# Attention scores as three fp16 products, with a tile's normalisation moved on VectorE

## The reference

```python
q, k, v = h @ Wq, h @ Wk, h @ Wv        # h = layernorm(x); 16 query heads, 4 key/value heads, 128 wide
qs, ks = softmax(q), softmax(k)         # over the 128 features
gl = log_sigmoid(k) / 16                # gate of the linear attention
sq, sk = rotary(q), rotary(k)
S_t = S_{t-1} * exp(gl_t)[:, None] + ks_t[:, None] * v_t[None, :]
o_gla = qs_t @ S_t                      # a scan over the tokens, one state per head
scores = sq @ sk.T * 128 ** -0.5        # causal mask, then softmax over the keys
y = softmax(scores) @ v
x = x + (0.5 * y + 0.5 * o_gla) @ Wo
x = x + moe(layernorm(x))               # router, 32 experts, top 4, capacity; and a shared expert
```

## Time and profile before

| | |
|---|---|
| runs | 2929.5, 2925.88, 2926.61 us, median 2926.61 |
| profiled execution | 2925.3 us, its span 2923.3 us |
| TensorE (PE) busy | 2656.4 us, 91% of the span |
| VectorE (DVE) busy | 1873.2 us, 64% |
| ScalarE (ACT) busy | 1502.2 us, 51% |
| GpSimd (POOL) busy | 1403.9 us, 48% |
| mean granted TensorE clock | 0.970 |

### The profile page before, as it was taken

The page is one execution under the profiler, slowest core; times in us unless marked ns, Lnnn a source line. Parts: engine busy times, 40 slices in busy tenths (PEclk is TensorE's granted clock), DMA queues, the critical chain, the costliest instruction groups (busy, mean ns, idle before and its releaser), DMA issues. The chain is left out here.

```text
span 2923.3 us, 50665 instructions
## 1 busy us (share of the span) xinstructions
PE 2656.4 (91%) x16228; PEld 1714.6 (59%) x16228; DVE 1873.2 (64%) x4603; ACT 1502.2 (51%) x4527; POOL 1403.9 (48%) x1495
## 2 busy tenths in 40 slices
PE   3899999999999999999999999999994899979872
PEld 2566666666666666666666666666653445447661
DVE  5666667666666666676667666666663677647661
ACT  4555555555555555555555555555542333337661
POOL 3445444544544454455445444544430466646653
PEclk9899999999999999999999999999997899989996
DMA  4500000000000000000000000000002221439995
GB/s 165 182 1 15 1 30 1 16 30 1 1 16 30 1 16 7 24 1 15 30 1 1 16 30 1 1 16 15 1 1 105 83 77 43 145 108 251 266 252 146
DMA packets 94018, 156.67 MB, mean 54 GB/s; under 512 B 13367, under 2 KB 47415, under 8 KB 92928
## 3 DMA queue, kind: packets, MB, share of 16 engines
q1 hardware_dynamic: 77296, 132.91, 14.1%
q0 software_dynamic: 16384, 16.33, 3.0%
q10 hardware_dynamic: 80, 4.19, 0.4%
HBM read 120.31 MB, written 81.40 MB: 69 GB/s over the span
## 5 line engine op out<-in xcount | busy, mean ns | idle before, releaser
L391 ACT ACTIVATE prob<-score_ps,neg_max 128x512 f32<-128x512 f32 (+3 forms) x512 | 271.1, 530 | 393.8 <-DVE neg_max L550 334.7
L275 POOL TENSOR_TENSOR parts<-qk,rope 128x640 f32<-128x640 f32 x128 | 197.1, 1540 | 411.2 <-issue 350.5
L747 PE MATMUL score_ps<-kr_t,qr_t 128*128 128x512 f32 (+3 forms) x1024 | 362.4, 445 | 7.8 <-ACT prob L391 7.7
L304 POOL TENSOR_TENSOR decay<-keys 128x512 f32<-128x512 f32 x128 | 134.1, 1047 | 365.3 <-DVE keys L598 365.3
L772 PE MATMUL out_ps<-prob_t,val 128*128 128x512 f32 (+3 forms) x1024 | 298.2, 434 | 9.7 <-ACT prob_t L397 9.7
L558 DVE TENSOR_SCALAR prob<-prob,inv_sum 128x512 f32<-128x512 f32 (+3 forms) x512 | 249.4, 487 | 18.0
L550 DVE TENSOR_REDUCE neg_max<-score_ps 128x1 f32<-128x512 f32 (+3 forms) x512 | 243.5, 485 | 24.5 <-PE score_ps L749 21.5
L772 PEld LDWEIGHTS out_ps<-prob_t,val 128*128 128x128 f32 x1024 | 185.6, 190 | 117.1 <-issue 61.2
L429 ACT ACTIVATE soft<-qk,neg_top 128x128 f32<-128x128 f32 x640 | 247.1, 387 | 6.0 <-DVE neg_top L572 2.5
L605 DVE TENSOR_TENSOR q_dec<-tr_ps,decay 128x512 f32<-128x512 f32 x128 | 88.2, 689 | 230.7 <-ACT decay L445 218.1
L814 PE MATMUL qkv_ps<-wq_high,x_t_high 128*128 128x512 f16 x512 | 196.3, 383 | 15.8 <-DVE wkv_low L498 15.8
(11 more groups left out here) (264 smaller groups left out, 7534.9 us busy)
## 6 DMA issues: line engine op xcount, KB each, us to landing
held_expert_w<-in_L_ffn_W_gate_dram SPq DMA_DIRECT2D x32, 512.0 KB
held_expert_w<-in_L_ffn_W_up_dram SPq DMA_DIRECT2D x32, 512.0 KB
held_expert_w<-in_L_ffn_W_down_dram SPq DMA_DIRECT2D x32, 512.0 KB, 7.7
rows<-const_empty_dram SPq DMA_DIRECT2D x1, 10560.0 KB, 39.9
e_xg<-rows SPq DMA_DIRECT2D x32, 330.0 KB
x_in<-_attn_hidden_states_dram SPq DMA_DIRECT2D x8, 1024.0 KB, 5.3
x_acc<-_attn_hidden_states_dram SPq DMA_DIRECT2D x8, 1024.0 KB, 5.3
x<-x_acc SPq DMA_DIRECT2D x8, 1024.0 KB, 4.4
```

What stands on the lines that cost most here:

```text
L275: nc.gpsimd.tensor_tensor(parts[:, 1, :].rearrange("p (h d) -> p h d", d=HALF), qk[:].rearrange("p (h d) -> p h d", d=HALF), rope[:, i, 1: ...
L304: nc.gpsimd.tensor_tensor(decay[:, 0:NSUB * P].rearrange("p (c s) -> p c s", s=P), mid.to_broadcast([P, NSUB, P]), run.unsqueeze(1).to_bro ...
L391: nc.scalar.activation(prob[:, i % 2, 0:w], score_ps[i % 2][:, 0:w], ACT.Exp, bias=neg_max[:, j:j + 1], accum_out=row_sum[:, j:j + 1]).the ...
L747: nc.tensor.matmul(score_ps[i % 2][:, 0:w], qr_t[p][:, h, i * P:(i + 1) * P], kr_t[p][:, 0:w], start=True, stop=False)
```

## The change

The rotated queries `qr_t` and keys `kr_t` are kept as two fp16 parts, high and low, in the same bytes as the fp32 tile before. ScalarE's two copies out of PSUM (L439, L442) now write the high part. A new function of VectorE, `turned_low`, writes what is left as the low part: one instruction for the keys (128 x 128) and one for the queries (128 x 512); it stands between `decays` and `apply_decays`, and in the tail between `decays` and the first `residual`. TensorE's fp32 score product becomes three fp16 products into the same PSUM tile. The semaphores `kr_t_ready` and `qr_t_ready`, which TensorE waits for, are now given by VectorE's instructions, and ScalarE's copies give two new ones, for which VectorE waits. And on VectorE `normalise(c, s + 1, 2)` moves behind `gate_logs` and `soften_keys` of the same iteration.

```diff
--- before.py
+++ after.py
@@ -62,8 +62,8 @@
         ident_b = sb("ident_b", [P, P], BF16)
         future_b = sb("future_b", [P, P], BF16)
 
-        qr_t = [sb(f"qr_t{n}", [P, G, SEQ]) for n in range(2)]
-        kr_t = [sb(f"kr_t{n}", [P, SEQ]) for n in range(2)]
+        qr_t = [sb(f"qr_t{n}", [P, 2, G, SEQ], FP16) for n in range(2)]
+        kr_t = [sb(f"kr_t{n}", [P, 2, SEQ], FP16) for n in range(2)]
         val = [sb(f"val{n}", [P, NT, DH]) for n in range(2)]
         q_in = [sb(f"q_in{n}", [P, G, SEQ - P]) for n in range(2)]
         local = [sb(f"local{n}", [P, NT, G, P]) for n in range(2)]
@@ -139,12 +139,14 @@
         soft_key_ready = sem("soft_key_ready")
         soft_query_ready = sem("soft_query_ready")
         keys_turned = sem("keys_turned")
+        kr_high_ready = sem("kr_high_ready")
         kr_t_ready = sem("kr_t_ready")
         keys_copied = sem("keys_copied")
         span_ready = sem("span_ready")
         diffs_ready = sem("diffs_ready")
         decay_ready = sem("decay_ready")
         queries_turned = sem("queries_turned")
+        qr_high_ready = sem("qr_high_ready")
         qr_t_ready = sem("qr_t_ready")
         soft_turned = sem("soft_turned")
         k_dec_ready = sem("k_dec_ready")
@@ -179,7 +181,8 @@
         def flat(t):
             return t.rearrange("p a b c -> p (a b c)") if len(t.shape) == 4 else t.rearrange("p a b -> p (a b)")
 
-        stage = [flat(t[:]) for t in (local[0], local[1], prob_t, x_acc, qr_t[1], qr_t[0])]
+        stage = [flat(t[:]) for t in (local[0], local[1], prob_t, x_acc)]
+        stage += [flat(qr_t[n][:]).bitcast(F32) for n in (1, 0)]
         wo_stage = stage[1:5]
         STAGES = len(stage)
 
@@ -436,11 +439,11 @@
                 act.wait_ge(q_in_ready, (NT - 1) * ua + max(i - 1, 0))
                 act.wait_ge(state_ready, (NT - 1) * ua + i)
                 nc.scalar.activation(span[:], tr_ps[0][:, 2 * P:4 * P], ACT.Exp).then_inc(span_ready, 1)
-                nc.scalar.activation(kr_t[p][:, i * P:(i + 1) * P], tr_ps[0][:, 0:P], ACT.Copy,
-                                     scale=float(DH) ** -0.5).then_inc(kr_t_ready, 1)
+                nc.scalar.activation(kr_t[p][:, 0, i * P:(i + 1) * P], tr_ps[0][:, 0:P], ACT.Copy,
+                                     scale=float(DH) ** -0.5).then_inc(kr_high_ready, 1)
                 act.wait_ge(queries_turned, a + 1)
-                nc.scalar.copy(qr_t[p][:, :, i * P:(i + 1) * P],
-                               tr_ps[1][:].rearrange("p (h t) -> p h t", t=P)).then_inc(qr_t_ready, 1)
+                nc.scalar.copy(qr_t[p][:, 0, :, i * P:(i + 1) * P],
+                               tr_ps[1][:].rearrange("p (h t) -> p h t", t=P)).then_inc(qr_high_ready, 1)
                 act.wait_ge(diffs_ready, a + 1)
                 nc.scalar.activation(decay[:], decay[:], ACT.Exp).then_inc(decay_ready, 1)
 
@@ -597,6 +600,15 @@
                 dve.wait_ge(k_dec_ready, a)
                 nc.vector.tensor_copy(keys[:], tr_ps[0][:, P:3 * P]).then_inc(keys_copied, 1)
 
+            def turned_low(a, i, p):
+                t = slice(i * P, (i + 1) * P)
+                dve.wait_ge(kr_high_ready, a + 1)
+                nc.vector.scalar_tensor_tensor(out=kr_t[p][:, 1, t], in0=tr_ps[0][:, 0:P], scalar=float(DH) ** -0.5,
+                                               in1=kr_t[p][:, 0, t], op0=ALU.mult, op1=ALU.subtract).then_inc(kr_t_ready, 1)
+                dve.wait_ge(qr_high_ready, a + 1)
+                nc.vector.tensor_tensor(qr_t[p][:, 1, :, t], tr_ps[1][:].rearrange("p (h t) -> p h t", t=P),
+                                        qr_t[p][:, 0, :, t], ALU.subtract).then_inc(qr_t_ready, 1)
+
             def apply_decays(a, ua, i, p):
                 dve.wait_ge(decay_ready, a + 1)
                 dve.wait_ge(local_done, a)
@@ -664,6 +676,7 @@
                         normalise(c, s, 0)
                     if prepare and s:
                         decays(NT * ua + s - 1)
+                        turned_low(NT * ua + s - 1, s - 1, p)
                         apply_decays(NT * ua + s - 1, ua, s - 1, p)
                     if c is not None:
                         if s < G - 1:
@@ -680,10 +693,11 @@
                         keep_local(NT * ua + s - 1, s - 1, p)
                     if c is not None and s < G - 1:
                         normalise(c, s + 1, 3)
-                        normalise(c, s + 1, 2)
                     if prepare:
                         gate_logs(NT * ua + s)
                         soften_keys(NT * ua + s)
+                    if c is not None and s < G - 1:
+                        normalise(c, s + 1, 2)
                     if more and g == KV - 2:
                         x_low(b + 1, s, tr_ps[min(s, 1)])
                     if more and g == KV - 3:
@@ -696,6 +710,7 @@
                     out_low(c, G - 1)
                 if prepare:
                     decays(NT * ua + NT - 1)
+                    turned_low(NT * ua + NT - 1, NT - 1, p)
                 if c is not None:
                     residual(c, b, g, PROJECTION[:2])
                 if prepare:
@@ -744,8 +759,9 @@
                     pe.wait_ge(x2_added[0], NT // 2 * c - 1)
                 else:
                     pe.wait_ge(x2_added[i % 2], NT // 2 * c)
-                nc.tensor.matmul(score_ps[i % 2][:, 0:w], qr_t[p][:, h, i * P:(i + 1) * P], kr_t[p][:, 0:w],
-                                 start=True, stop=False)
+                for n, (q_, k_) in enumerate(THREE):
+                    nc.tensor.matmul(score_ps[i % 2][:, 0:w], qr_t[p][:, q_, h, i * P:(i + 1) * P], kr_t[p][:, k_, 0:w],
+                                     start=(n == 0), stop=False)
                 nc.tensor.matmul(score_ps[i % 2][:, i * P:w], future_b[:], ident_b[:], start=False,
                                  stop=True).then_inc(scores_done, 1)
```

## The result

The changed kernel takes **2972.2 us** (median of four runs, 2969.4 to 2977.1), the kernel before 2926.2 us beside it (2922.7 to 2929.5). The ratio is 1.0159, with a 95% interval of 1.0146 to 1.0172: slower by 46 us, forecast 2974. The profiled execution has a span of 2969.4 us and a mean granted TensorE clock of 0.97, as before.

A forecast was written before the change was run, and what follows sets the result against it. A ring of waits through VectorE, GpSimd and ScalarE bounds iterations 1 and 2, TensorE the rest. 31 x (2.55 - 0.50 - 0.36) = 52 us, less 4, less about 1, gives +47: 2974 us, range 2946 to 3000.

The forecast's parts named there:

- What bounds the kernel: A ring of waits through VectorE, GpSimd and ScalarE bounds iterations 1 and 2; TensorE bounds the rest.
- TensorE had room for it: At g = 1, 0.61 us more on VectorE lengthened the keys-to-keys ring by 0.56; TensorE could absorb that.
- TensorE's part: Three fp16 products for one fp32 score product: 0.50 us at a unit's start plus 0.36 in iteration 1, 0.86 gained.
- the step with the row maxima: In iteration 1 the next head's scores end sooner, so VectorE's second row maximum can start 0.36 us sooner.
- from the tail to the next unit: At a unit's start the scores of tiles 3, 2 and 1 get 0.22 + 0.17 + 0.11 = 0.50 us shorter.
- The moved normalisation: The moved 384-wide product meets GpSimd's soften_queries: VectorE's chain grows 0.85 us in iterations 0, 1 and 2, 2.55 per unit.
- The rival that the port goes to VectorE first: VectorE gets in ahead of GpSimd: +0.25 us in each of three iterations, 2918 us; chance 0.08.
- What comes back at g = 2: The 256-wide product most likely misses other GpSimd work: 3 x 0.19 us in 7 units, 4 us back.
- The low parts: VectorE's two new rows per block fit into the wait for decay, and in the tail before the residual: cost nothing.
- The rival of two iterations: The price falls in two iterations, iteration 0 having unseen room: 2948 us; counted as lower edge within the forecast's 0.78.
- The sum: 31 x (2.55 - 0.50 - 0.36) = 52 us, less 4, less about 1 in the last unit: +47 us.
- One sign: In the changed profile, TensorE would be less busy by some 70 us.

The follow-up runs named there:

- e6: The kernel before with one 256-wide VectorE row added ahead of the 512-wide normalisation in iterations 0 to 2: 2962.3 us, ratio 1.0127.
- e5: The changed kernel with the normalisation where it was and only the high x high score product, the other two left out: 2889.8 us, ratio 0.9882.
- e7: The kernel before with 0.22 us of TensorE matmuls added ahead of the scores of tile 1, for heads 1 and 2: 2931.0 us, ratio 1.0017.
- e1: The changed kernel with the normalisation back where it was, so the fp16 score products alone: 2898.1 us, ratio 0.9909.
- e3: The changed kernel with GpSimd's soften_queries also waiting until the moved 384-wide product is done: 2919.4 us, ratio 0.9981.
- e4: The changed kernel without VectorE's low-part rows; all three score products read the high parts: 2970.0 us, ratio 1.0154.
- e2: The kernel before, fp32 scores kept, with only the normalisation moved: 3000.2 us, ratio 1.0254.
- e8: e1 with GpSimd's second half of the rotation held back until the keys' softmax row is done: 2913.9 us, ratio 0.9959.

## Why the prediction was right, point by point

- **What bounds the kernel.** Right in kind: e6 charges VectorE's row in full, and the steps of the loop move by 0.11 us and nothing in e5, where TensorE loses 1.1 us of products per head (2 x 1280 columns at 0.216 us for 512). Too generous in one place: "TensorE had room for it" was read at g = 1, and holds there; at g = 0 and 3 e7 finds 0.06 us of room.
- **TensorE's part**, -0.86 us per unit. From before to e1 a unit gets 1.01 us shorter at g = 0, 0.97 at g = 1, 0.95 at g = 2 and 0.80 at g = 3. The terms too: 0.38 in the step with the row maxima (0.36 forecast), 0.57 from the tail to the next unit (0.50 forecast). Over the 31 units that makes about 28 us, where 31 x 0.86 gave 27; two units lose 1.26 us again to the clock, the last unit gives 1 us, and the run is 27 us shorter. That e1 meets its forecast to the microsecond is in part luck: a gain that was slightly larger than forecast and a loss that nobody forecast.
- **The moved normalisation**, +0.85 us in three iterations: after minus e1, 0.84, 0.85 and 0.84 at g = 0, 2.53 per unit against 2.55. Start and end of the gate, of `soften_queries` and of the moved product lie within 0.01 us of the forecast times. The rival that the port goes to VectorE first falls with e3, which shows what that would look like: 0.25. What spoke for it, the short 512-wide product, has another reason: that product starts before GpSimd's L288 and shuts L288 out, which is then 1.05 us long instead of 0.86 (the last section has the counts). The Trainium skill (SBUF — State Buffer, "SBUF: two separate sides"), that whoever starts first has the port for the whole instruction, would give 1.04. GpSimd's L296 ends at 1234.47, and the product that it shuts out at 1234.69, though alone it takes 0.42 us: 0.20 us of its own work lies beside the blocking row. The measurement decides for 0.85. The page's list of the rows concerned fits: `q_dec`, which has one input in PSUM, always runs beside GpSimd work and is never longer than 0.69 us; and `o_t_low`, of the same width and also from PSUM, takes 0.67 to 0.69 us with GpSimd work beside it and without.
- **What comes back at g = 2.** After minus e1 is 0.66 us in both steps there instead of 0.85, and 0.66 from the tail of g = 1 into it: 0.57 per unit, as the 3 x 0.19 of the sum.
- **The low parts**: nothing, by e4; their times in the trace are the forecast ones (0.29 and 0.69 us, end at 1240.60, `q_dec` 0.50 us later). In the tail the residual did not wait for them.
- **The rival of two iterations** falls with the table: iteration 0 pays as well.
- **The sum**: forecast +47, measured +46. By the steps of the 31 units the move is worth +74 (forecast 75, with the 4 us that come back at g = 2) and the products -28 (forecast -27), and the last unit is 0.95 us shorter (forecast about 1), so that the terms meet their forecasts and not only the sum. One sign was off: TensorE's busy time fell by 41.3 us (2656.4 to 2615.0), not 70. The rows of the score products alone shrank from 362.4 to 284.8 us over the whole span. The busy time of all rows together fell less, and it is no measure of the work: e2, with the same TensorE work as the kernel before, shows 2674.9 us, 18.5 more. A possible reason: fp16 rows of 512 columns are shown 0.38 us long and start 0.216 us apart, so that short waits lie under the end of the row ahead. That reason is argued, not tested.

## What to carry to other kernels

When a row is moved on VectorE, look up what GpSimd does at its new place *and* what takes its old one: the price here was 0.60 us for the row that came to stand beside another GpSimd instruction, and 0.25 for the row that inherited the old collision. Find the ring of waits before counting an engine's busy time; an engine at 98% can have room, and one at 66% be the pace. Make the two halves of a change apart: here a gain of 27 us lay under a loss of 75.

## What the runs showed of the hardware

- A VectorE row shut out by GpSimd is not merely put off. It ends less than its own length behind GpSimd's row: 0.22 us for the 384-wide product (0.42 alone), 0.15 for the 128-wide gate (0.28 alone), the same to 0.01 us in every long row of every kernel. For the product it is 0.15 at 256 columns (0.35 alone) and 0.28 at 512 (0.49 alone), so some 0.20 us of it is not paid again, at each of the three widths. e6 shows it at 512 columns, where the added row pushed the normalisation into GpSimd's rows:

```profile
L559 DVE TENSOR_SCALAR prob<-prob,inv_sum 128x512 f32<-128x512 f32 x115 | 100.2, 871 | 4.1
```

  With 871 ns instead of the 549 of the kernel before, it paid while the 384-wide product behind it, now clear of them, came down to 455 from the 735 of the earlier trace rows. A collision moves from row to row, and the sum of the two stays nearly the same.
- The shutting out goes both ways, and of these rows the one that started first is held up little or not at all (the 512-wide product takes 0.52 us there, 0.49 alone). From 165 to 2105 us, GpSimd's second half of the rotation (L288) is 1.04 to 1.06 us long in all 87 places of the kernel before where a VectorE product runs at its start, and 0.86 or 0.87 us in all 117 of e8, where none does. In e6 the added row puts the product behind the start of GpSimd's row (there L289), and the roles change (timelines of VectorE and GpSimd in e6):

```profile
1225.24 1.01 DVE L559 TENSOR_SCALAR prob<-prob,inv_sum 128x512 f32<-128x512 f32 x1
1225.12 0.86 POOL L289 TENSOR_TENSOR rot<-parts 128x320 f32<-128x320 f32 x1
```

- Less TensorE work can lower its clock. e5 left out 0.43 us of products per head at 512 columns, and the clock went to its lower level at every change of sequence, after waits such as 1.10 and 1.24 us with little work between. With three products instead of one it did so twice in e1, three times in e3, once in e8, and never in the change and in e4; in the kernel before it never did. So the same TensorE work can fall on either side.
